# State-space loop of a decoder kernel: a step product in a buffer for each block, the channels' SiLU two units sooner, the first decay ahead, half of the C rows ahead of the locked sum

## The chip, the cores and the metric

The kernel runs on one core of a Trainium2 chip. The time is that of one execution on the device, in microseconds (us). Five engines run side by side, each through its own list of instructions in order, and wait for one another with semaphores: TensorE (PE, matmuls), VectorE (DVE), ScalarE (ACT), GpSimd (POOL) and SyncE (SP, which here only issues DMAs).

## The reference

Two decoder layers on x of 16 x 64 tokens by 256. Each layer is a mixer, a cross attention and a feed-forward part, all with a residual. The change lies in the first mixer alone, a state-space block with 512 channels and 16 states:

```python
zxbcdt = hidden_states @ W_in.T
z, x, Bm, Cm, dtl = jnp.split(zxbcdt, splits, axis=-1)
dt_full = dtl @ W_dt.T + b_dt
delta = jax.nn.softplus(dt_full + b_dt)
...
x = jax.nn.silu(x + conv_b[None, :, None])       # after a causal convolution over 4 steps
...
def step(state, inp):
    u, dlt, Bs, Cs = inp
    dA = jnp.exp(dlt.reshape(b, NC, DPG)[..., None] * A_g)
    du = (dlt * u).reshape(b, NC, DPG)
    state = dA * state + du[..., None] * Bs[:, :, None, :]
    y = jnp.einsum('bgdn,bgn->bgd', state, Cs).reshape(b, D_INNER)
    return (state, y)
...
y = y + x.transpose(0, 2, 1) * D_param
y = y * jax.nn.silu(z)
return y @ W_out.T
```

Here `x` after the SiLU is `u` in the kernel, `dlt` is delta, `dA` the decay, `du` the step product.

## The kernel before

The 512 channels lie in four blocks k = 0 to 3 (`NK`) of 128 partitions; a row of a tile holds all 1024 tokens (`TOK`). The 16 states are walked one at a time (`DST`), so the loop has 64 units u = 16k + n. What one unit does, engine by engine:

- ACT, L637: the decay `m_da` of unit u, exp(delta times a column of `a_log`), in a ring of three buffers; it waits for scan u-3. In three units of a block, n = 4, 9, 14 (`SHARED`), also L643, the `put`: it copies a finished input row into PSUM.
- PE, L1083 (`put_b`): for the other 13 units two selecting matmuls that spread row B of the unit over the partitions into PSUM; `put_b(u+1)` stands in iteration u and waits for scan u-1. L1095 (`add_state`): adds `m_hc` of unit u-2 to the block's y in PSUM banks 4 and 5, with four passes of 512 columns in the profile.
- DVE, L1869: the product B times `m_du` for units that have their own (52 of 64). L1874: the scan over time, h = dA h + input. Scan u waits for `m_hc` of unit u-3, since `m_h` is a ring of three.
- POOL, L468: `m_hc` = h times the row of C. For shared units L473: it multiplies the loaded row B by `m_du`, three units ahead (`m_pd`).
- SP, L318: loads `m_cb`, the unit's rows of C spread over the partitions (512 KB), in a ring of three; the load for unit u is issued when `m_hc` of unit u-3 is done. Shared units also load `m_bb` (512 KB), four units ahead.

Beside this, block k+1 is made ready during block k. PE (L1047, `project`) makes dt in n = 0 and 1 (`steps`), C in n = 3 and 4 (`columns`), the convolution in n = 11 and z of block k in n = 13 and 14. From n = 0 on, all of them but the x columns and the convolution use PSUM banks 6 and 7 in turn. ACT reads dt in L583 and L584 (`step_in`, n = 2, signalled by `m_ax`), then makes the softplus, copies the C rows (L576, n = 6), takes up the convolution (L612, n = 12), computes u by SiLU at the end of n = 15 (L616, `channels`) and right behind it SiLU of z (L668), then loads the exponential's table set again (L553). POOL has the softplus pieces (L434, L438, L444 at n = 12), the step product `m_du` (L452, `step_inputs`, ahead of the `m_hc` of n = 14) and the gate (L458, n = 4 of the next block). DVE adds the skip term after the third scan of the next block (L1850, `skip`); the first `add_state` of that block (L1095, n = 0) waits for it with `m_yd`, since it starts banks 4 and 5 anew. This is the locked sum.

`m_du` is one tile, in `region_c`; `ctxT`, the transposed context for the cross attention behind the loop, is loaded at the start of the program, and `m_rowsT` holds the C rows of a block on their way to DRAM. The order on each engine is the written order; no scheduler changes it. In what follows sum16 means `add_state(16)`, put17 `put_b(17)`, hc13 the `m_hc` of unit 13, and so on; du1 is the step product of block 1.

## Time and profile before

| | us |
|---|---|
| median of 3 runs | 925.9 |
| lowest and highest | 923.86 and 926.99 |
| the profiled execution, its own time | 924.2 |
| its span | 922.3 |
| busy in the span: PE, DVE, ACT, POOL | 822.4, 549.7, 433.7, 302.3 |

The span is what the profiler saw from the first to the last instruction; 1.9 us lie around it. The loop runs from 41.5 us (first scan) to 275.6 us (last scan) of this span, some 25% of it. The large PE share belongs to the stages behind the loop. In a timeline row stand the start, the duration (of a merged group from its first start to its last end), engine, line, operation, written tile and read tiles, and in brackets how long the engine sat idle before and what the profile holds responsible. That releaser is inferred from the last semaphore event, and an instruction waiting for several can be put down to the wrong one. The end of a PE group is modelled; how far apart two groups start is the safer measure.

### The profile page before, as it was taken

The page shows a single profiled execution, that of the slowest core. Times are in us where ns is not written, and L with a number is a line of the kernel's source. Part 1 is how long each engine was busy: PE and PEld are TensorE (multiplying, and loading weights), DVE is VectorE, ACT ScalarE, POOL GpSimd, SP SyncE. Part 2 cuts the span into 40 slices and gives each one's busy share as a digit, 9 for nine tenths or more (in the row PEclk, how much of TensorE's full clock was granted, in tenths as well). Part 3 has the DMA queues.
Part 4 walks back from the last instruction along what each step waited for, and adds up shares of the span by engine and source line. Part 5 has one row for each costly group of instructions (what it writes and reads, how often), then busy time and mean ns, then how long its engine had stood idle before and what let it go on. Part 6 is the DMA issues. An engine that isn't in the chain of part 4 may idle for free.

```text
span 922.3 us, 12515 instructions
## 1 busy us (share of the span) xinstructions
PE 822.4 (89%) x5082; PEld 502.2 (54%) x5082; DVE 549.7 (60%) x666; ACT 433.7 (47%) x650; POOL 302.3 (33%) x148
## 2 busy tenths in 40 slices
PE   6797897986989889999999899998989799989977
PEld 2232342332445456666666676666677466657755
DVE  3799989899895223333424534347792534565686
ACT  2774566545433555555564321233654222232475
POOL 0089999899880000000001001111017993000000
PEclk9889899899899999999999999999999999999999
DMA  9576666656994200000000121405100000000001
GB/s 309 149 190 175 179 163 179 185 173 173 246 229 154 108 1 1 1 1 1 1 1 12 41 92 64 177 18 192 69 3 1 1 1 1 1 1 1 1 1 46
DMA packets 26376, 77.02 MB, mean 84 GB/s; under 512 B 3568, under 2 KB 10480, under 8 KB 25072
## 3 DMA queue, kind: packets, MB, share of 16 engines
q1 hardware_dynamic: 25552, 74.13, 27.4%
q0 software_dynamic: 768, 2.10, 0.7%
q8 instruction: 41, 0.67, 0.3%
q14 instruction: 15, 0.12, 0.0%
HBM read 68.75 MB, written 7.08 MB: 82 GB/s over the span
## 4 chain that ended last, share of the span: by engine, by line
PE 56%; ACT 11%; DVE 11%; DMA 9%; POOL 7%; issue 6%; SPq 0%; POOLq 0%; DVEq 0%; ACTq 0%
PE ps L1297 11%; PE ps L1213 9%; DMA region_b<-m_rows 5%; POOL region_c L468 4%; PE ps L1396 4%; PE ps L1422 4%; PE ps L1285 4%; PE ps L1260 4%; DMA region_c<-m_rows 3%; PE ps L1218 2%; PE ps L1095 2%; PE ps L1047 2%; POOL region_b L468 2%; PE ps L1166 2%; PE ps L1465 2%
## 5 line engine op out<-in xcount | busy, mean ns | idle before, releaser
L1213 PE MATMUL ps<-xnT,region_a 128*128 128x512 f32 x256 | 120.1, 599 | 1.4 <-ACT region_c L718 0.8
L468 POOL TENSOR_TENSOR region_c<-region_c,region_b 128x1024 f32<-128x1024 f32 x42 | 100.9, 2410 | 54.6 <-DMA region_b<-m_rows 47.5
L1095 PE MATMUL ps<-region_c,ident 128*128 128x512 f32 x168 | 90.0, 665 | 17.2 <-POOL region_c L468 11.0
L1874 DVE TENSOR_TENSOR_SCAN region_c<-region_c,ps 128x1024 f32<-128x1024 f32 x43 | 97.9, 2283 | 1.7 <-ACT ps L643 0.4
L489 POOL DMA_INDIRECT f_in<-xn,f_row x8 | 8.0, 995 | 277.2 <-DVE f_row L1985 275.4
L1951 DVE COPY region_b<-ps 128x512 f32<-128x512 f32 x32 | 21.4, 689 | 83.7 <-PE ps L1271 83.6
L1213 PEld LDWEIGHTS ps<-xnT,region_a 128*128 128x128 f32 x256 | 47.2, 190 | 41.2 <-issue 35.8
L1869 DVE TENSOR_TENSOR ps<-ps,region_c 128x1024 f32<-128x1024 f32 x52 | 63.3, 1217 | 10.3 <-PE ps L1083 10.3
L1095 PEld LDWEIGHTS ps<-region_c,ident 128*128 128x128 f32 x168 | 34.2, 212 | 58.0 <-issue 33.6
L1297 PE MATMUL ps<-region_c 128*128 128x256 f32 x256 | 59.8, 380 | 0.0
L1297 PEld LDWEIGHTS ps<-region_c 128*128 128x128 f32 x256 | 48.5, 190 | 16.7 <-issue 11.5
L468 POOL TENSOR_TENSOR region_b<-region_c 128x1024 f32<-128x1024 f32 x21 | 50.6, 2408 | 8.4 <-DVE region_c L1874 5.9
L637 ACT ACTIVATE region_c<-region_c,a_log 128x1008 f32<-128x1008 f32 x43 | 47.9, 1127 | 9.1 <-DVE region_c L1874 9.0
L1095 PE MATMUL ps<-region_b,ident 128*128 128x512 f32 x84 | 44.7, 658 | 8.1 <-POOL region_b L468 6.0
L1874 DVE TENSOR_TENSOR_SCAN region_c<-region_a,ps 128x1024 f32<-128x1024 f32 x21 | 48.0, 2283 | 3.1 <-issue 1.4
L710 ACT ACTIVATE region_c<-ps 128x512 f32<-128x512 f32 x32 | 19.1, 596 | 64.9 <-PE ps L1213 64.9
L1047 PE MATMUL ps<-xnT,region_b 128*128 128x512 f32 (+1 forms) x96 | 47.4, 629 | 0.7 <-ACT xnT L544 0.7
L713 ACT ACTIVATE region_c<-ps 128x512 f32<-128x512 f32 x32 | 19.1, 596 | 57.5 <-PE ps L1213 57.5
L1083 PE MATMUL ps<-region_b,sel_b 96*128 96x512 bf16 x104 | 33.7, 409 | 14.0 <-DVE region_c L1874 14.0
L746 ACT ACTIVATE region_c<-ps 128x512 f32<-128x512 f32 x48 | 25.5, 598 | 35.5 <-PE ps L1285 35.5
L1916 DVE TENSOR_TENSOR region_c<-ps,small 128x1024 f32<-128x1024 f32 x8 | 9.8, 1225 | 54.1 <-PE ps L1260 54.1
L1285 PE MATMUL ps<-region_b,ctxn 64*128 64x256 f32 x256 | 38.4, 433 | 3.7 <-ACT region_c L746 2.5
(252 smaller groups left out, 1636.3 us busy)
## 6 DMA issues: line engine op xcount, KB each, us to landing
region_b<-m_rows SPq DMA_DIRECT2D x43, 512.0 KB, 5.1
region_c<-m_rows SPq DMA_DIRECT2D x21, 512.0 KB, 5.1
xn<-m_brows SPq DMA_DIRECT2D x12, 512.0 KB, 4.3
region_a<-in_x_wo SPq DMA_DIRECT2D x2, 2048.0 KB, 10.9
m_rows<-region_b SPq DMA_DIRECT2D x4, 512.0 KB, 5.5
region_a<-in_x_wq SPq DMA_DIRECT2D x8, 256.0 KB, 7.2
region_b<-in_f_fc SPq DMA_DIRECT2D x1, 2048.0 KB, 7.9
region_b<-in_f_proj SPq DMA_DIRECT2D x1, 2048.0 KB, 13.1
```

What stands on the lines that cost most here:

```text
L468: pool.tensor_tensor(m_hc[u % 3], m_h[u % 3], m_cb[u % 3], ALU.mult).then_inc(sem("m_hc"), 1)
L637: act.activation(m_da[u % 3][:, :, 1:S], m_delta[k % 2][:, :, 1:S], ACT.Exp, scale=a_log[:, k, n:n + 1]).then_inc(sem("m_da"), 1)
L1047: last = pe.matmul(ps[0:rows, pair_at + c, :], lhs(k), (rhs if rhs is not None else xnT[:, k, :])[:, c * HALF:c * HALF + HALF], start=(k = ...
L1095: last = pe.matmul(ps[:, 4 + c, :], ident[:, :], m_hc[u % 3][:, c * HALF:c * HALF + HALF], start=(n == 0), stop=(n == DST - 1))
L1213: last = pe.matmul(b, w, xnT[:, k, cols(it)], start=(k == 0), stop=(k == KH - 1))
L1260: last = pe.matmul(ps[64 * (b % 2):64 * (b % 2) + 64, 4 + a // 2, c:c + S], q_T[:, a, S * b:S * b + S], keys_T[:, S * b:S * b + S], start= ...
L1285: last = pe.matmul(banks[r].rearrange("p (s a q) -> p s a q", s=2, a=4)[:, s], ctxn[64 * r:64 * r + 64, 4 * (it // 4) + 2 * m + s, :], mov ...
L1297: last = pe.matmul(tiles2(2 * (it // 4) + t // 2)[:, t % 2, :], o_Ts[layer][it % 2][:, a, 128 * t:128 * t + 128], wvo[layer][:, 4 * (it % ...
L1396: last = pe.matmul(ps[:, 4 + 2 * (s % 2) + c, :], f_xT[h][:, j, k, :], f_fc[:, bass.ds(weights_at[s] + (HID * k + HALF * c), HALF)], start ...
L1422: last = pe.matmul(ps[:, 2, 0:D], f_aT[s % 2][:, hb, :], f_proj[:, bass.ds(weights_at[s] + D * hb, D)], start=(hb == 0), stop=(hb == HB - 1))
L1869: dve.tensor_tensor(inputs(u), inputs(u), m_du, ALU.mult).then_inc(sem("m_dbu"), 1)
L1874: dve.tensor_tensor_scan(m_h[u % 3], m_da[u % 3].rearrange("p b t -> p (b t)"), inputs(u), 0.0, ALU.mult, ALU.add).then_inc(sem("m_scan"), 1)
```

## The change

1. `m_du` becomes a list of four: blocks 0 and 2 in the old tile, block 1 in `ctxT`, block 3 in `m_rowsT`. So du of the next block no longer waits for this block's last products; block 2 waits for block 0's, block 3 for the last store of C rows.
2. The load of `ctxT` goes from the start of the program to unit (k = 3, n = 2), behind the C rows of that unit.
3. POOL makes du ahead of the `m_hc` of n = 13, not of n = 14.
4. ACT computes u (`channels`) at n = 13, with its own change of tables and back; at n = 15 it makes the first decay of the next block ahead of SiLU of z.
5. PE makes the first half of the C columns at n = 2 ahead of `add_state`, which there is the locked sum; the second half stays at n = 3.

```diff
-        m_du = view("C", 56, [TOK])
+        m_du = [view("C", 56, [TOK]), ctxT[:, :], view("C", 56, [TOK]), m_rowsT]
...
-            load(ctxT[:, :], io["ctxT"], "ld_x0")
...
                     if n == 2:
                         sp.wait_ge(sem("m_delta"), NK)
                         sp.wait_ge(sem("m_u"), NK)
+                        sp.wait_ge(sem("m_pd"), len(SHARED) * (NK - 2))
+                        sp.wait_ge(sem("m_dbu"), own_products(DST * (NK - 2) - 1))
+                        load(ctxT[:, :], io["ctxT"], "ld_x0")
...
             def step_inputs(k):
                 pool.wait_ge(sem("m_u"), k + 1)
                 pool.wait_ge(sem("m_delta"), k + 1)
-                pool.wait_ge(sem("m_pd"), len(SHARED) * k)
-                pool.wait_ge(sem("m_dbu"), own_products(DST * k - 1))
-                pool.tensor_tensor(m_du, m_delta[k % 2].rearrange("p b t -> p (b t)"), m_u[:, k, :], ALU.mult)\
+                if k == 2:
+                    pool.wait_ge(sem("m_pd"), len(SHARED))
+                    pool.wait_ge(sem("m_dbu"), own_products(DST - 1))
+                if k == 3:
+                    pool.wait_ge(sem("st_rows"), 16 * NK)
+                pool.tensor_tensor(m_du[k], m_delta[k % 2].rearrange("p b t -> p (b t)"), m_u[:, k, :], ALU.mult)\
                     .then_inc(sem("m_du"), 1)
...
-                if n == DST - 2 and k < NK - 1:
+                if n == DST - 3 and k < NK - 1:
                     step_inputs(k + 1)
...
+            for u in range(NK * DST):
+                k, n = u // DST, u % DST
+                if n or not k:
+                    decay(u)
...
+                    if n == DST - 3:
+                        channels(k + 1)
+                        exp_tables()
                     if n == DST - 1:
-                        channels(k + 1)
+                        decay(u + 1)
...
+                if n == 2 and k < NK - 1:
+                    pe.wait_ge(sem("m_ax"), k + 2)
+                    columns("C", k + 1, (0,))
                 if u >= 2:
                     add_state(u - 2)
...
-                    if n in (3, 4):
-                        pe.wait_ge(sem("m_ax"), k + 2)
-                        columns("C", k + 1, (n - 3,))
+                    if n == 3:
+                        columns("C", k + 1, (1,))
```

`decay(u)` is the old code of L637 with its waits, put into a function. The products of DVE and POOL name `m_du[k]` in place of `m_du`. Three places show the new order. In the listings a name in brackets is a semaphore that the instruction waits for.

POOL at the end of block 0, from hc11 to the first of block 1; L468 is `m_hc`, L473 the product for a shared unit, L444 the end of delta, L452 du. Before:

```order
L468 TENSOR_TENSOR region_b<-region_c 128x1024 [waits m_y,ld_cb2,m_scan]
L473 TENSOR_TENSOR xn<-xn,region_c 128x1024 [waits ld_bb0,m_du]
L468 TENSOR_TENSOR region_c<-region_c,region_b 128x1024 [waits m_y,ld_cb0,m_scan]
L444 TENSOR_TENSOR region_c<-region_a 128x1024 [waits m_sel]
L468 TENSOR_TENSOR region_c<-region_c,region_b 128x1024 [waits m_y,ld_cb1,m_scan]
L452 TENSOR_TENSOR region_c<-region_c 128x1024 [waits m_pd,m_dbu,m_delta,m_u]
L468 TENSOR_TENSOR region_b<-region_c 128x1024 [waits m_y,ld_cb2,m_scan]
```

In the changed kernel `m_hc` is L473, the shared product L478, the end of delta L446 and du L457:

```order
L473 TENSOR_TENSOR region_b<-region_c 128x1024 [waits m_y,ld_cb2,m_scan]
L478 TENSOR_TENSOR xn<-xn,region_c 128x1024 [waits ld_bb0,m_du]
L473 TENSOR_TENSOR region_c<-region_c,region_b 128x1024 [waits m_y,ld_cb0,m_scan]
L446 TENSOR_TENSOR region_c<-region_a 128x1024 [waits m_sel]
L457 TENSOR_TENSOR ctxT<-region_c 128x1024 [waits m_delta,m_u]
L473 TENSOR_TENSOR region_c<-region_c,region_b 128x1024 [waits m_y,ld_cb1,m_scan]
L473 TENSOR_TENSOR region_b<-region_c 128x1024 [waits m_y,ld_cb2,m_scan]
```

du has changed places with hc13, and hc13 stands behind it.

ACT from the take-up of the convolution (L612) to the first decay of block 1; L637 is the decay, L643 the copy of a shared row, L616 SiLU for u, L668 SiLU of z, L553 the table set of the exponential. Before:

```order
L612 ACTIVATE region_a<-ps,mpar 128x1024 [waits m_proj]
L637 ACTIVATE region_a<-region_c,a_log 128x16x63 [waits m_scan]
L637 ACTIVATE region_c<-region_c,a_log 128x16x63 [waits m_scan]
L643 ACTIVATE ps<-xn 128x1024 [waits m_scan,m_pd]
L637 ACTIVATE region_c<-region_c,a_log 128x16x63 [waits m_scan]
L616 ACT_TABLE_LOAD
L616 ACTIVATE region_c<-region_a 128x1024 [waits m_conv]
L668 ACTIVATE region_c<-ps 128x1024 [waits m_delta,m_yg,m_proj]
L553 ACT_TABLE_LOAD
L637 ACTIVATE region_a<-region_c,a_log 128x16x63 [waits m_scan,m_delta]
```

In the changed kernel these lines are L617, L642, L653, L621, L681 and L558:

```order
L617 ACTIVATE region_a<-ps,mpar 128x1024 [waits m_proj]
L642 ACTIVATE region_a<-region_c,a_log 128x16x63 [waits m_scan]
L621 ACT_TABLE_LOAD
L621 ACTIVATE region_c<-region_a 128x1024 [waits m_conv]
L558 ACT_TABLE_LOAD
L642 ACTIVATE region_c<-region_c,a_log 128x16x63 [waits m_scan]
L653 ACTIVATE ps<-xn 128x1024 [waits m_scan,m_pd]
L642 ACTIVATE region_c<-region_c,a_log 128x16x63 [waits m_scan]
L642 ACTIVATE region_a<-region_c,a_log 128x16x63 [waits m_scan,m_delta]
L681 ACT_TABLE_LOAD [waits m_delta,m_yg]
L681 ACTIVATE region_c<-ps 128x1024 [waits m_proj]
L558 ACT_TABLE_LOAD
```

SiLU for u with a load on either side now stands ahead of the decay and the copy of unit 14, and SiLU of z behind the first decay of block 1.

PE from put19 to put21, in block 1; L1083 is `put_b`, L1095 `add_state`, L1047 the C columns. Before:

```order
L1083 MATMUL ps<-region_b,sel_b 128x512 [waits m_scan]
L1083 MATMUL ps<-region_b,sel_b 128x512
L1095 MATMUL ps<-region_c,ident 128x512 [waits m_yd,m_hc]
L1095 MATMUL ps<-region_c,ident 128x512
L1095 MATMUL ps<-region_b,ident 128x512 [waits m_hc]
L1095 MATMUL ps<-region_b,ident 128x512
L1047 MATMUL ps<-xnT,region_b 128x512 [waits m_ax]
L1047 MATMUL ps<-xnT,region_b 128x512
L1083 MATMUL ps<-region_b,sel_b 128x512 [waits m_scan]
```

In the changed kernel they are L1096, L1108 and L1060:

```order
L1096 MATMUL ps<-region_b,sel_b 128x512 [waits m_scan]
L1096 MATMUL ps<-region_b,sel_b 128x512
L1060 MATMUL ps<-xnT,region_b 128x512 [waits m_ax]
L1060 MATMUL ps<-xnT,region_b 128x512
L1108 MATMUL ps<-region_c,ident 128x512 [waits m_yd,m_hc]
L1108 MATMUL ps<-region_c,ident 128x512
L1108 MATMUL ps<-region_b,ident 128x512 [waits m_hc]
L1108 MATMUL ps<-region_b,ident 128x512
L1060 MATMUL ps<-xnT,region_b 128x512 x2
L1096 MATMUL ps<-region_b,sel_b 128x512 [waits m_scan]
```

One half of C stands ahead of the locked sum and the other ahead of put21, so both halves now stand between put19 and put21, where only one stood. The half that stood between put21 and put22 is gone from there.

## Rows read from the trace of the kernel before

**Rows 1.** Busy time by stretch: us and instructions of each engine, clock, DMA share

```profile
98.40:159.30 60.90, 52.17 (x123) 21.28 (x122) 55.88 (x32) 37.76 (x37) 56.88 (x25) 0.94 0.66 173
...
220.00:282.00 62.00, 51.22 (x136) 23.73 (x135) 56.87 (x37) 23.56 (x22) 48.70 (x21) 0.94 0.93 243
```

**Rows 2.** Timeline of DVE at the block edges and around the locked sum

```profile
91.30 2.26 DVE L1874 TENSOR_TENSOR_SCAN region_c<-region_a,ps 128x1024 f32<-128x1024 f32 x1
...
98.44 1.23 DVE L1869 TENSOR_TENSOR ps<-ps,region_c 128x1024 f32<-128x1024 f32 x1 [1.44 <-PE ps L1083]
...
101.91 1.21 DVE L1869 TENSOR_TENSOR ps<-ps,region_c 128x1024 f32<-128x1024 f32 x1
...
118.05 1.23 DVE L1869 TENSOR_TENSOR ps<-ps,region_c 128x1024 f32<-128x1024 f32 x1 [1.51 <-PE ps L1083]
...
121.92 1.23 DVE L1869 TENSOR_TENSOR ps<-ps,region_c 128x1024 f32<-128x1024 f32 x1 [0.32 <-PE ps L1083]
...
152.13 2.26 DVE L1874 TENSOR_TENSOR_SCAN region_c<-region_c,ps 128x1024 f32<-128x1024 f32 x1
...
159.26 1.23 DVE L1869 TENSOR_TENSOR ps<-ps,region_c 128x1024 f32<-128x1024 f32 x1 [1.43 <-PE ps L1083]
...
220.07 1.23 DVE L1869 TENSOR_TENSOR ps<-ps,region_c 128x1024 f32<-128x1024 f32 x1 [1.41 <-PE ps L1083]
```

**Rows 3.** Timeline of POOL: hc13 and du1, then hc51

```profile
93.56 2.37 POOL L468 TENSOR_TENSOR region_c<-region_c,region_b 128x1024 f32<-128x1024 f32 x1
95.88 2.36 POOL L452 TENSOR_TENSOR region_c<-region_c 128x1024 f32<-128x1024 f32 x1
...
235.75 2.35 POOL L468 TENSOR_TENSOR region_c<-region_c,region_b 128x1024 f32<-128x1024 f32 x1 [1.63 <-PE ps L1095]
```

**Rows 4.** Timeline of PE: sum13 to put21, then the same place at the later edges

```profile
95.99 1.98 PE L1095 MATMUL ps<-region_c,ident 128*128 128x512 f32 x4
97.81 0.60 PE L1083 MATMUL ps<-region_b,sel_b 96*128 96x512 bf16 x2
100.61 3.54 PE L1095 MATMUL ps<-region_b,ident 128*128 128x512 f32 x4 [2.21 <-POOL region_b L468]
103.94 1.21 PE L1047 MATMUL ps<-region_a,region_b 128*128 128x512 f32 x2
...
110.50 3.13 PE L1095 MATMUL ps<-region_c,ident 128*128 128x512 f32 x4 [1.90 <-DVE region_c L1850]
...
115.70 1.88 PE L1047 MATMUL ps<-xnT,region_b 128*128 128x512 f32 x4
117.42 0.60 PE L1083 MATMUL ps<-region_b,sel_b 96*128 96x512 bf16 x2
...
161.44 2.92 PE L1095 MATMUL ps<-region_c,ident 128*128 128x512 f32 x4 [2.21 <-POOL region_c L468]
...
222.24 1.98 PE L1095 MATMUL ps<-region_c,ident 128*128 128x512 f32 x4 [2.21 <-POOL region_c L468]
```

**Rows 5.** Timeline of PE: a group behind 1.78 us of idle time

```profile
70.96 0.61 PE L1083 MATMUL ps<-region_b,sel_b 96*128 96x512 bf16 x2 [1.78 <-DVE region_c L1874]
```

**Rows 6.** Timeline of ACT: units 13 to 15, step_in of block 2, copy of unit 30

```profile
85.02 1.12 ACT L637 ACTIVATE region_c<-region_c,a_log 128x1008 f32<-128x1008 f32 x1
...
89.03 1.03 ACT L643 ACTIVATE ps<-xn 128x1024 f32<-128x1024 f32 x1 [1.86 <-POOL xn L473]
...
91.13 1.28 ACT L616 ACT_TABLE_LOAD   x1
92.42 1.06 ACT L616 ACTIVATE region_c<-region_a 128x1024 f32<-128x1024 f32 x1
...
109.21 1.11 ACT L584 ACTIVATE region_a<-ps,mpar 128x1024 f32<-128x1024 f32 x1
...
149.84 1.03 ACT L643 ACTIVATE ps<-xn 128x1024 f32<-128x1024 f32 x1 [3.41 <-POOL xn L473]
```

**Rows 7.** DMA issues: KB each, median us from issue to landing

```profile
region_b<-m_rows SPq DMA_DIRECT2D x43, 512.0 KB, 5.1
```

8 lines of the change are left out of this document (4 added, 4 removed).

## The prediction

> **What bounds the kernel now.** I began with the busy time by stretch [rows 1]. Between the first products of blocks 1 and 2 DVE is busy for 55.88 of 60.90 us and POOL for 56.88. Both are nearly full, and PE with 52.17 of modelled busy time is not far off. The change touches only the loop, so what it can give lies in the few microseconds in which DVE idles there. The timeline of DVE [rows 2] shows where: 1.44, 1.43 and 1.41 us ahead of the first product of blocks 1, 2 and 3 (I call these places the edges), then 1.51 and 0.32 us ahead of products 21 and 22. Block 2 repeats the last two as 1.51 and 0.32 ahead of products 37 and 38; block 3, which makes no C for a next block, has no such pair.
>
> The releaser in the first of these rows is misleading. put16 was done before sum13 started at 95.99 [rows 4], while du1 on POOL ran from 95.88 to 98.24 [rows 3] and product 16 started at 98.44. The edge waits for du, and du stands behind hc13 in POOL's list. Product 21 starts 0.63 us behind the start of put21 (117.42), and put21 stands behind sum16, sum17 and half a C; this chain starts when the skip term releases sum16 at 110.50 [rows 4]. So the edge belongs to POOL and the second place to PE.
>
> In every sum below I use distances between starts, since the ends on PE are modelled. A group of four passes at full clock takes 1.72 us (C half, 115.70 to 117.42) or 1.82 behind a wait (sum13, 95.99 to 97.81). At the lower clock level sum14 took 3.33 (100.61 to 103.94); the same place at the next edge lasts 2.92 as a row, and 1.98 at the third, where the clock stayed up. A row outlasts the distance by 0.16 to 0.2, so the three prices are 3.33, about 2.7 and 1.82 [rows 4].
>
> **Part 1: du ahead of hc13, with a tile for each block.** The new tiles remove the wait for product 15, which ends where scan 15 starts, some 2.3 before 97.0, and would hold du at its new place. du now starts where hc13 did, at 93.56, and ends at 95.9, ahead of the end of scan 15 at 97.0 (98.44 less 1.44) [rows 2, 3]. The idle 1.44 ahead of product 16 goes, three times, 4.3 us in all. What is late next is hc13: it ends at 98.24 in place of 95.93. Two things wait for it. Scan 16 could start at 98.24, when product 16 is through, so it loses at most 0.1. And PE: sum13 stands ahead of put17 in PE's list. Before, sum13 ran at 95.99 and PE idled for 2.21 us behind put17; now PE idles for some 2.4 us ahead of sum13, and put17 starts at 98.3 plus one group. That is 100.1, 101.0 or 101.6 for the three prices, and product 17 at 0.63 more: 100.7, 101.6 or 102.3. It started at 101.91 [rows 2], so the edge yields +1.2, +0.3 or -0.4 us instead of 1.44. Since 2.4 us of idle time is longer than the 2.21 behind which the clock fell at two edges of three, I take the middle, +0.3, and keep both ends.
>
> hc14 to hc16 keep their places in time. The C rows of unit 16 are asked for when hc13 is done, now 2.3 us later: at about 98.7, landing 5.1 later [rows 7] at 103.8, where POOL would want them at 102.9. POOL then runs 0.9 late, but over the block it idled for 4.0 us [rows 1], and sum16 waits for the skip and not for hc16. Nothing on the path.
>
> **Part 2: SiLU for u two units sooner.** At n = 13 ACT now has, behind the decay of 85.02, a table load 1.28, SiLU 1.06 and a load back 1.28 [rows 6], 3.6 us, ahead of the decay and the copy of unit 14. The cover is ACT's wait of 1.86 for the shared product ahead of that copy. The copy thus ends at about 91.9 instead of 90.06, and scan 14, which started at 91.30 [rows 2], starts at about 92.0: 0.7 late in block 0. In block 1 the wait ahead of the copy is 3.41 [rows 6]: the copy moves by 0.2 to 0.3 and is through at 151.1, scan 30 starts at 152.13 [rows 2]. Nothing is lost there, and block 2 stands alike. In block 0 the 0.7 comes out of the 1.44 that DVE would wait at the edge, so product 17 can't be sooner than 101.1; it costs nothing unless put17 is at its quickest. POOL has u long before du's new place. The Trainium skill, page "ScalarE: Activation LUTs", section "What ACT_TABLE_LOAD costs", adds a drain of about 1380 ns to each load of 1283 ns. This trace shows the 1.28 but no drain: the load starts at 91.13 and SiLU at 92.42 [rows 6]. By the page the copy would be another 2.8 us late; that is a rival below.
>
> **Part 3: the first decay ahead of SiLU of z.** Without it the decay of unit 16 would stand behind SiLU of z and a table load and would be the next wait of scan 16. Now it follows the decay of 15 and is done by about 95. It makes Part 1 possible, no more. SiLU of z has a load of its own again, in the time in which ACT waits for z. Zero.
>
> **Part 4: the C half ahead of the locked sum.** It looks as if 1.9 us of PE's idle time ahead of sum16 took up a group of 1.72. But the half needs `m_ax`, since dt lies in the same banks, and the second instruction of `step_in` runs from 109.21 to 110.32 [rows 6], just when the skip is done too. So the half doesn't go into that idle time as it stands. Moreover both halves now stand ahead of put21: from PE's restart R to put21 there are four groups, 6.9 us at full clock, where three took 6.92 (110.50 to 117.42), for sum16 and sum17 ran in part at the lower level (5.20 from 110.50 to 115.70 against 3.44, 1.8 us too much) [rows 4]. Gain or loss thus hangs on two questions.
>
> When is R? The edge moves it. With sum14 no longer the group behind the wait, the dt halves and `m_ax` come sooner: sum14 starts at about 101.4 and takes 1.72, so it ends at 103.1 in place of 103.94, and the first dt half loses its slow share, 0.2 (a row of 1.21, where half a group and the 0.16 by which rows outlast the distance are 1.02). R is 110.3 less 1.0, 109.3. At the cheap edge it is 108.7, at the dear one 110.0.
>
> And the clock? The idle time ahead of R is 1.7 us. Behind 1.90 the groups ran at the lower level, behind 1.78 at the higher (0.61 for a put, as at full clock) [rows 4, 5]. I take the higher: 109.3 + 6.9 = 116.2 for put21 against 117.42, 1.2 us. As the half is gone ahead of put22, DVE's 0.32 there goes too: 1.5 in block 1. Block 2 is the same with 1.4. These two sums already hold the gain of their edge, because it is PE that releases product 21. With the lower level, 1.8 dearer, each becomes -0.3.
>
> **Part 5: ctxT.** It leaves a time at the start in which nothing behind it was waited for and comes into block 3, where the DMAs are busy for 0.93 of the time at 243 GB/s [rows 1]. 512 KB are 2.1 us there. POOL stands still for 1.63 us at that time [rows 3] (hc51 waits for the skip by way of sum48), so the C rows of unit 52 may be 0 to 0.5 us late; I take 0.3. The waits of SP for it are all over by then.
>
> **The sum.** Block 1 -1.5, block 2 -1.4, edge of block 3 -0.3, ctxT +0.3: -2.9 us. From the profiled execution, 924.2 (its span 922.3), that is 921.3. The median of the runs is 925.9, 1.7 above that execution, so 923.0. About 0.3%, 2.8 us, is what a measurement of this kernel can tell from no change; the forecast lies right on that bound.
>
> **The rivals.** *The clock stays up at the edges too* (for it: the third edge; against: the first two). Then R is 108.7, put21 at 115.6, so 2.2 and 2.3 for the blocks and 1.2 for the third edge: 5.7 less 0.3, and 920.5. *The idle time of 1.7 costs the lower level* (for it: 1.90 did, twice): 0.3 lost in both blocks, the third edge and ctxT cancel, 0.6 slower: 926.5. *The C half is uncovered, slower*: if `m_ax` comes no sooner than before, R stays at 110.3, and at the lower level put21 comes 6.9 + 1.8 later, at 119.0, 1.6 late; 0.3 comes back at product 22. Twice 1.3, with 0.4 lost at the third edge and 0.5 for ctxT: 3.5 slower, 929.4. It decides from the point at which the second half of dt ends no sooner than 108.1 (the first instruction of `step_in`, 1.0, stands between it and 109.21). *A table change dearer than its row*: with a second 1.3 for each load the copies of units 14 and 30 are 2.6 us later, scan 14 is 3.3 and scan 30 some 1.7 late, and the edges can't repay it; about 3 slower, 929. That is the page's case.
>
> **How the numbers follow.** Forecast, R sooner at the higher clock and the edges in part: 0.45, from 921 to 925, half of it beyond the bound. Clock up everywhere: 0.20. Lower level at R: 0.20. Uncovered half: 0.12. Dear tables: 0.02, with 0.01 for anything else. Faster by over 0.3%: 0.23 + 0.20 = 0.43. Slower: 0.11. Within: 0.46. The range reaches to the best rival and beyond the third, 919.8 to 927.5, and leaves out the two slow ones and a little below.
>
> **What would show it.** DVE: no idle time ahead of products 16, 32 and 48, but 0.2 to 1.8 ahead of products 17, 33 and 49, put down to PE. POOL: the du rows ahead of hc13. PE: an idle time of 2.4 ahead of sum13, and of 1.7 ahead of the first C half; two groups for C between put19 and put21. DVE's wait ahead of product 21 still about 1.2 and that ahead of 22 gone. ACT: six table loads more in the loop, scan 14 about 0.7 late and scans 30 and 46 in time. I am wrong if put17 isn't held by sum13, if the first C half starts while PE would have idled before, or if the clock's levels fall otherwise than where the rows of before have them.

## The result, and the profile after

The change made the kernel slightly slower. Over 20 runs each on one chip the changed kernel took 926.92 us in the median and the kernel before 924.73; the ratio is 1.0031, interval 1.0017 to 1.0045. Between the medians lie 2.2 us more, where 2.9 us less was forecast. One execution of the kernel before took 1200.73 us, far from all others, and does not enter the ratio.

| | before | after |
|---|---|---|
| the profiled execution | 924.2 | 922.14 |
| its span | 922.3 | 920.2 |
| busy in it: PE, DVE, ACT, POOL | 822.4, 549.7, 433.7, 302.3 | 814.0, 549.4, 441.7, 302.4 |
| mean granted clock in it | 0.963 | 0.974 |
| first scan to last scan | 231.89 | 230.99 |

The profiled execution of the changed kernel is the quickest of its twenty (922.14 to 933.93), so its trace shows the change at its best: the loop takes 0.9 us less than in the trace of the kernel before, while the medians lie 2.2 us the other way. Even there something is given back. From the last scan to the end the program took from 646 to 654 us in the twenty traces of this document, so spans and loops of single traces are compared with care, and the ratios rest on the many executions.

Busy time by stretch, for blocks 1 and 3 of the changed kernel, from first product to first product and from product 48 on (columns as in [rows 1]):

```profile
96.16:156.46 60.30, 50.40 (x122) 20.63 (x122) 55.69 (x33) 40.36 (x39) 56.85 (x25) 0.97 0.65 174
215.24:277.00 61.76, 50.21 (x130) 22.20 (x131) 53.88 (x33) 24.49 (x23) 50.31 (x22) 0.97 0.96 240
```

Block 1 is 0.6 us shorter than in [rows 1], with the same work on DVE and POOL. In block 3 the share of the DMAs is 0.96 where it was 0.93; the load of ctxT itself now lies there.

DVE of the changed kernel (start, duration; the idle time ahead in brackets): products 16, 17, 21, 22 and 48 with scan 16, which answer to [rows 2], then scans 52, 56, 57 and 62.

```profile
96.16 1.21 DVE L1884 TENSOR_TENSOR ps<-ps,ctxT 128x1024 f32<-128x1024 f32 x1
97.78 2.29 DVE L1889 TENSOR_TENSOR_SCAN region_c<-region_c,ps 128x1024 f32<-128x1024 f32 x1 [0.42 <-POOL region_c L473]
101.37 1.23 DVE L1884 TENSOR_TENSOR ps<-ps,ctxT 128x1024 f32<-128x1024 f32 x1 [1.30 <-PE ps L1096]
...
117.22 1.23 DVE L1884 TENSOR_TENSOR ps<-ps,ctxT 128x1024 f32<-128x1024 f32 x1 [1.43 <-PE ps L1096]
...
120.69 1.21 DVE L1884 TENSOR_TENSOR ps<-ps,ctxT 128x1024 f32<-128x1024 f32 x1
...
215.24 1.21 DVE L1884 TENSOR_TENSOR ps<-ps,region_b 128x1024 f32<-128x1024 f32 x1
...
231.69 2.29 DVE L1889 TENSOR_TENSOR_SCAN region_c<-region_c,ps 128x1024 f32<-128x1024 f32 x1 [0.84 <-ACT ps L653]
...
247.32 2.29 DVE L1889 TENSOR_TENSOR_SCAN region_c<-region_a,ps 128x1024 f32<-128x1024 f32 x1 [1.88 <-ACT region_a L642]
251.13 2.29 DVE L1889 TENSOR_TENSOR_SCAN region_c<-region_c,ps 128x1024 f32<-128x1024 f32 x1 [1.52 <-ACT ps L653]
...
268.60 2.29 DVE L1889 TENSOR_TENSOR_SCAN region_c<-region_a,ps 128x1024 f32<-128x1024 f32 x1 [1.40 <-ACT ps L653]
```

The edges' waits are gone and so is the 0.32 ahead of product 22. Product 48 starts 4.8 us sooner than before (220.07). Then come waits that the kernel before does not have: scans 52, 57 and 62 wait for the copy (L653) of a shared row, 0.84 + 1.52 + 1.40 = 3.8 us.

POOL of the changed kernel at the first edge: du1, hc13, then hc16, hc17 and the shared product of unit 20. Below it the third edge: hc48 and hc49 as one row, then the shared product of unit 52.

```profile
92.99 2.35 POOL L457 TENSOR_TENSOR ctxT<-region_c 128x1024 f32<-128x1024 f32 x1
95.31 2.34 POOL L473 TENSOR_TENSOR region_c<-region_c,region_b 128x1024 f32<-128x1024 f32 x1
...
104.19 2.35 POOL L473 TENSOR_TENSOR region_c<-region_c,region_b 128x1024 f32<-128x1024 f32 x1 [1.91 <-DMA region_b<-m_rows]
106.50 2.35 POOL L473 TENSOR_TENSOR region_b<-region_c 128x1024 f32<-128x1024 f32 x1
108.80 2.37 POOL L478 TENSOR_TENSOR xn<-xn,ctxT 128x1024 f32<-128x1024 f32 x1
...
223.64 4.65 POOL L473 TENSOR_TENSOR region_c<-region_c,region_b 128x1024 f32<-128x1024 f32 x2 [2.29 <-PE ps L1108]
228.26 2.34 POOL L478 TENSOR_TENSOR xn<-xn,region_b 128x1024 f32<-128x1024 f32 x1
```

And the kernel before at its third edge: hc48, hc49 and the same shared product.

```profile
224.47 2.34 POOL L468 TENSOR_TENSOR region_c<-region_c,region_b 128x1024 f32<-128x1024 f32 x1
227.14 2.35 POOL L468 TENSOR_TENSOR region_c<-region_c,region_b 128x1024 f32<-128x1024 f32 x1 [0.34 <-DVE region_c L1874]
229.45 2.35 POOL L473 TENSOR_TENSOR xn<-xn,region_c 128x1024 f32<-128x1024 f32 x1
```

Before, hc48 started 3.1 us behind the start of scan 48 (221.33), right behind hc47, and no edge had a wait for a DMA. After, hc48 starts 6.8 us behind scan 48 (216.83), and the shared product of unit 52 stands 11.4 us behind that scan instead of 8.1. The 2.29 ahead of hc48 is put down to PE, which had long been done; the same instruction at the first edge is put down to its C rows. The copy of unit 52 on ACT follows the shared product, and scan 52 follows the copy.

### The profile page after: what moved, and what is told of

Its sections match the earlier page's. It is cut to its first block, busy times and chain, and to the rows that moved or that the text cites. A ratio compares the mean times of both kernels' runs of the same rounds, so it can differ in the third digit from the quotient of the medians.

```text
span 920.2 us, 12520 instructions
## 1 busy us (share of the span) xinstructions
PE 814.0 (88%) x5082; PEld 496.6 (54%) x5082; DVE 549.4 (60%) x666; ACT 441.7 (48%) x656; POOL 302.4 (33%) x148
## 4 chain that ended last, share of the span: by engine, by line
PE 52%; ACT 8%; DVE 8%; DMA 6%; issue 2%; POOL 1%; another core or an unknown queue 0%; SPq 0%; DVEq 0%; ACTq 0%; POOLq 0%
PE ps L1312 11%; PE ps L1228 9%; PE ps L1411 4%; PE ps L1437 4%; DMA region_b<-m_rows 4%; PE ps L1275 4%; PE ps L1300 4%; PE ps L1233 2%; DMA region_c<-m_rows 2%; PE ps L1181 2%; PE ps L1286 1%; PE ps L1480 1%; ACT region_c L759 1%; PE ps L1533 1%; PE ps L1189 1%
## 5 line engine op out<-in xcount | busy, mean ns | idle before, releaser
L473 POOL TENSOR_TENSOR region_c<-region_c,region_b 128x1024 f32<-128x1024 f32 x42 | 100.8, 2407 | 55.0 <-DMA region_b<-m_rows 45.9
L1108 PE MATMUL ps<-region_c,ident 128*128 128x512 f32 x168 | 85.9, 638 | 19.8 <-POOL region_c L473 16.0
L1108 PEld LDWEIGHTS ps<-region_c,ident 128*128 128x128 f32 x168 | 31.5, 197 | 59.0 <-issue 29.5
L642 ACT ACTIVATE region_c<-region_c,a_log 128x1008 f32<-128x1008 f32 x43 | 48.2, 1129 | 15.3 <-DVE region_c L1889 10.6
L473 POOL TENSOR_TENSOR region_b<-region_c 128x1024 f32<-128x1024 f32 x21 | 50.5, 2404 | 6.3 <-DMA region_c<-m_rows 2.9
L1060 PE MATMUL ps<-xnT,region_b 128*128 128x512 f32 (+1 forms) x96 | 48.5, 640 | 4.2 <-ACT region_a L589 3.5
L1096 PE MATMUL ps<-region_b,sel_b 96*128 96x512 bf16 x104 | 32.6, 398 | 16.9 <-DVE region_c L1889 16.9
L1108 PE MATMUL ps<-region_b,ident 128*128 128x512 f32 x84 | 41.1, 611 | 6.0 <-POOL region_b L473 5.9
L1953 DVE TENSOR_TENSOR region_c<-region_c 128x1024 f32<-128x1024 f32 x8 | 9.8, 1222 | 46.9 <-ACT region_c L718 46.9
```

What stands on the lines that cost most here:

```text
L473: pool.tensor_tensor(m_hc[u % 3], m_h[u % 3], m_cb[u % 3], ALU.mult).then_inc(sem("m_hc"), 1)
L642: act.activation(m_da[u % 3][:, :, 1:S], m_delta[k % 2][:, :, 1:S], ACT.Exp, scale=a_log[:, k, n:n + 1]).then_inc(sem("m_da"), 1)
L1060: last = pe.matmul(ps[0:rows, pair_at + c, :], lhs(k), (rhs if rhs is not None else xnT[:, k, :])[:, c * HALF:c * HALF + HALF], start=(k = ...
L1108: last = pe.matmul(ps[:, 4 + c, :], ident[:, :], m_hc[u % 3][:, c * HALF:c * HALF + HALF], start=(n == 0), stop=(n == DST - 1))
```

## The experiments

Every kernel computes the whole reference, and every ratio is against the kernel before on the same chip, from 12 executions of the kernel and 23 to 35 of the kernel before (20 each for the first); the interval is one of 95%. Kernels of one set ran on one chip and are to be compared within it. "Lag" is the DVE time in front of scans 52, 57 and 62 put down to the copy of a shared row, in the one traced execution; the last column is in us, of that execution too.

| set, kernel | ratio | interval | lag | first to last scan |
|---|---|---|---|---|
| the changed kernel | 1.0031 | 1.0017 to 1.0045 | 3.76 | 230.99 |
| 1 after_again | 1.0044 | 1.0020 to 1.0069 | 0 | 233.74 |
| 1 ctxt_behind | 1.0017 | 0.9992 to 1.0042 | 1.37 | 235.51 |
| 1 c_in_place | 1.0030 | 1.0003 to 1.0057 | 0.65 | 235.22 |
| 1 before_ctxt_late | 1.0000 | 0.9976 to 1.0025 | 0.52 | 229.08 |
| 2 after_fence | 1.0029 | 1.0009 to 1.0048 | 0 | 230.94 |
| 2 before_fence | 0.9995 | 0.9977 to 1.0012 | 0 | 229.92 |
| 2 after_fence_ctxt_behind | 1.0002 | 0.9979 to 1.0025 | 2.79 | 231.36 |
| 2 du_in_place | 0.9988 | 0.9969 to 1.0007 | 0 | 227.82 |
| 3 du_in_place_again | 0.9988 | 0.9970 to 1.0007 | 0 | 231.09 |
| 3 cb_first | 0.9995 | 0.9976 to 1.0014 | 0 | 227.91 |
| 3 cb_first_ctxt_behind | 0.9989 | 0.9971 to 1.0007 | 1.03 | 229.60 |
| 3 du_and_c_in_place | 0.9999 | 0.9980 to 1.0018 | 0.31 | 230.32 |
| 4 after_third | 1.0015 | 0.9988 to 1.0042 | 2.33 | 235.90 |
| 4 cb_first_again | 0.9974 | 0.9950 to 0.9998 | 0 | 229.74 |
| 4 before_cb_first | 0.9983 | 0.9957 to 1.0009 | 0.47 | 229.75 |
| 4 du_in_place_cb_first | 0.9974 | 0.9945 to 1.0003 | 0 | 228.08 |
| 5 after_fourth | 1.0023 | 1.0002 to 1.0045 | 5.09 | 233.31 |
| 5 after_fence_again | 1.0025 | 1.0008 to 1.0043 | 4.08 | 233.43 |

The letters in an expectation are that set's own names for the theories that it weighs.

### Set 1: the load of ctxT, the C half

after_again is the changed kernel unaltered. The edits of the others:

```diff
 # ctxt_behind: the changed kernel, ctxT loaded behind the loop
-                        sp.wait_ge(sem("m_pd"), len(SHARED) * (NK - 2))
-                        sp.wait_ge(sem("m_dbu"), own_products(DST * (NK - 2) - 1))
-                        load(ctxT[:, :], io["ctxT"], "ld_x0")
...
+            load(ctxT[:, :], io["ctxT"], "ld_x0")
             load(wvT, io["x0_wvT"], "ld_x0")
```

```diff
 # c_in_place: the changed kernel, both C halves where they were
-                if n == 2 and k < NK - 1:
-                    pe.wait_ge(sem("m_ax"), k + 2)
-                    columns("C", k + 1, (0,))
...
-                    if n == 3:
-                        columns("C", k + 1, (1,))
+                    if n in (3, 4):
+                        pe.wait_ge(sem("m_ax"), k + 2)
+                        columns("C", k + 1, (n - 3,))
```

```diff
 # before_ctxt_late: the kernel before, ctxT loaded in unit (3, 2)
-            load(ctxT[:, :], io["ctxT"], "ld_x0")
...
                         sp.wait_ge(sem("m_u"), NK)
+                        load(ctxT[:, :], io["ctxT"], "ld_x0")
```

> The changed kernel once more, to see how its executions spread. Theory L (the load of ctxT in block 3 makes the C rows late, and that eats the gain): 1 to 4 us slower than before, with DVE idle for some 3 to 6 us in block 3 ahead of scans 52 to 62, whatever the clock does. Theory K (the higher clock of the trace shown, 0.974, was luck): other executions have a mean granted clock near 0.965, and lower-level groups behind the idle time ahead of the first C half, which cost 1 to 2 us in blocks 1 and 2. Both can hold together.

> The changed kernel with the load of ctxT moved out of block 3 to just behind the loop, ahead of the load of wvT. Theory L: 3 to 5 us faster than the changed kernel, so 1 to 3 us faster than before; the C rows of block 3 land 5 to 7 us after their issue as before and not 8 to 9. Theory K: no different from the changed kernel within 1 us.

> The changed kernel with both C halves at n = 3 and 4 behind the locked sum, as before. Theory K: 1 to 3 us faster than the changed kernel, if the half ahead of the sum is what costs. Theory L: equal to it, or up to 1 us slower, since the two kernels make product 21 wait by about the same (three groups at the lower clock level or four at the higher).

> The kernel before with only one thing changed: ctxT is loaded at unit (k = 3, n = 2), behind the C rows. Theory L: 2 to 4 us slower than before. Theory K: equal to before within 1 us.

The loss came again, 1.0044. Without the 512 KB in block 3 some of it may be missing (1.0017, with overlapping intervals), yet the same load does nothing that can be measured to the kernel before (1.0000). The C half in its old place does not undo the loss either (1.0030). So neither is the cause alone.

The traces of after_again, ctxt_behind and c_in_place have one predicated copy on DVE of 8.0 us where the others take 3.4. It lies beside POOL. Here is the plainest case, from after_third, a later run of the changed kernel: DVE's copy, then POOL's instructions beside it (hc42 and hc43 in one row, the shared product of unit 46, hc44).

```profile
199.86 8.02 DVE L1861 COPY_PREDICATED region_a<-region_a,region_b 128x1024 f32<-128x1024 uint32 x1 [0.57 <-POOL region_b L440]
```

```profile
199.69 4.65 POOL L473 TENSOR_TENSOR region_c<-region_c,region_b 128x1024 f32<-128x1024 f32 x2
204.31 2.35 POOL L478 TENSOR_TENSOR xn<-xn,region_c 128x1024 f32<-128x1024 f32 x1
211.40 2.36 POOL L473 TENSOR_TENSOR region_b<-region_c 128x1024 f32<-128x1024 f32 x1 [4.75 <-DVE region_c L1889]
```

POOL runs from 199.69 to 206.66 without a gap, and the copy ends 1.2 us behind that. Was this the cause?

### Sets 2 and 5: no copy beside POOL

```diff
 # after_fence, after_fence_again, before_fence; with the edit of ctxt_behind: after_fence_ctxt_behind
+                if n == 11 and k < NK - 1:
+                    pool.wait_ge(sem("m_sel"), k + 1)
                 pool.wait_ge(sem("m_scan"), u + 1)
```

`m_sel` is signalled by the copy, so POOL starts hc11, hc27 and hc43 only when the copy is through.

> The changed kernel, and POOL waits ahead of the m_hc of n = 11 until DVE's predicated copy is done. Theory P (the copy reads three SBUF operands and shares a port with POOL; when it misses the gap between two POOL instructions it waits for three of them and takes 8.0 us and not 3.4, and that is what makes typical executions of the change slower): no copy of 8 us in the trace, 1.5 to 3 us faster than the changed kernel, so 0 to 1 us slower than before or faster, and a smaller spread. Rival Q (the long copies are rare and the kernel before has as many; the change is slower for its C rows and tables): equal to the changed kernel, 2 to 3.5 us slower than before.

> The kernel before with the same wait of POOL for the copy. Theory P, if only the change brings the long copies: equal to before within 1 us. If the kernel before has them too, 1 to 2 us faster than before. Rival Q: as the latter.

> The changed kernel with POOL's wait for the copy, and ctxT loaded behind the loop. Theory P with the C rows of block 3 costing too: the fastest of the set, 2 to 4 us faster than before. If the load of ctxT costs nothing once the copies are short: equal to after_fence. Rival Q: 1 to 2 us slower than before, as without the wait.

> The changed kernel beside the next one on one chip: 1.0015 to 1.0045 of before, as the three times before. Its trace may have one copy of 8.0 us where the others have 3.4.

> The changed kernel with POOL waiting for the predicated copy ahead of hc11, so that no copy can run against it. If the late C rows cost their time mainly at the edges and behind them, it is level with after_fourth within 0.12%. If they cost it mainly through the long copies (4.6 us each, in most executions), it is 0.25 to 0.4% below after_fourth.

The nine copies in the fenced traces with du early all take 3.4 us. The loss stays: 1.0029, and 1.0025 beside 1.0023 of the unfenced kernel on one chip. So keeping the long copies away does not bring the time back. They occur in 4 of 18 copies in the unfenced traces with du early and the loads in their order, in none of 9 with the C rows issued first, and in none of 21 with du in its old place or in the kernel before without the fence.

That does not clear the long copies of every share. From scan 14 to product 49 the two unfenced traces of the changed kernel that hold one take 134.04 and 133.94 us (after_again, after_third), the two without take 128.69 and 128.42 (the first one, after_fourth): some 5.4 us less. But the three fenced traces take 130.97 to 131.32 there. In them PE idles 2.8 us ahead of sum13, sum29 and sum45, where it idles 2.5 to 2.6 otherwise, so the fence seems to have a price of its own with du early; in the kernel before it has none (0.9995). And the late C rows cost time without a long copy as well: after_fourth has no long copy and 5.09 us of lag, while after_again has one and no lag. How the loss is divided between the two stays open.

### Sets 2 and 3: du back behind hc13, and the C rows sooner

```diff
 # du_in_place, du_in_place_again; with the edit of c_in_place: du_and_c_in_place
-                if n == DST - 3 and k < NK - 1:
+                if n == DST - 2 and k < NK - 1:
                     step_inputs(k + 1)
```

```diff
 # cb_first, cb_first_again; with the edit of ctxt_behind: cb_first_ctxt_behind
+                load(m_cb[u % 3], m_rows[k][8 * n:8 * n + 8].partition_broadcast(DST), f"ld_cb{u % 3}")
                 if u + 4 < NK * DST and shared(u + 4):
...
                     load(m_bb[j % 2], m_brows[u + 4:u + 5].partition_broadcast(128), f"ld_bb{j % 2}")
-                load(m_cb[u % 3], m_rows[k][8 * n:8 * n + 8].partition_broadcast(DST), f"ld_cb{u % 3}")
```

In units 16, 32 and 48 SP issues the shared row of the unit four ahead, and behind it the C rows. Both wait for the `m_hc` of three units before, which is hc13, hc29 and hc45: the very instruction that du was put in front of.

> The changed kernel with du on POOL ahead of the m_hc of n = 14, as before; tiles, tables, decay and C halves as changed. My sum gave the edges about 0.3 us each and the rest to the C halves, so 1 to 2 us slower than the changed kernel if nothing else counted. If du's place is what brings long copies (theory P in its narrow form): no copy of 8 us, and 1 to 2 us faster than the changed kernel.

> du in its old place once more, on the chip of the runs beside it. Theory D (making du two positions sooner makes hc13 and with it the load of the next block's first C rows 2.3 us late; POOL waits for them at every edge, 1.9 to 2.5 us, and that is the loss): 1 to 3 us faster than before again, 3 us faster than the changed kernel; in the trace no POOL wait for C rows at the edges, and a loop of 228 us or so. Rival N (the earlier result was the chip's spread): equal to before or slower.

> The changed kernel, with the load of a unit's C rows issued ahead of the load of the shared B row, where both come in one unit (among them the first unit of each block). It takes 512 KB and one issue out of the way of the late C rows and keeps du sooner. Theory D: POOL's wait of 1.9 to 2.5 us at the edges falls to under 1, and the kernel is 1.5 to 3 us faster than the changed one, about equal to before. Rival R (the loss comes from PE, where sum13 holds put17 back, and not from the C rows): equal to the changed kernel within 1 us, with DVE still waiting ahead of products 17, 33 and 49.

> As cb_first, and ctxT loaded behind the loop. Theory D with DMA time short in block 3: 3 to 4 us faster than the changed kernel, 1 us faster than before. Rival R: 1 to 2 us slower than before, as with ctxT behind alone.

> du and both C halves in their old places; what is left of the change is the tiles, the tables, the decay ahead and the late ctxT. By my sum for the C halves (1.2 us in each of two blocks when the clock stays up, a loss of 0.3 when it falls): 0 to 2.5 us slower than with du alone in place. These edits without du sooner and without the C half should be worth nothing by themselves: equal to before within 1 us.

The rest of the change, without du early, is at 0.9988 twice. The unfenced changed kernel did not run on that chip; against after_fence, which did, du_in_place is 0.41% faster by the means (interval 0.19 to 0.63%), of which the fence may account for a part. du_and_c_in_place came 1.1 us behind du_in_place_again by the means, inside the noise and inside what was expected, and level with the kernel before. du_in_place, POOL with hc17 and the shared product of unit 20, then DVE with products 16 and 21, then PE with the first C half and put21:

```profile
104.96 2.35 POOL L473 TENSOR_TENSOR region_b<-region_c 128x1024 f32<-128x1024 f32 x1 [0.40 <-DVE region_c L1889]
107.28 2.36 POOL L478 TENSOR_TENSOR xn<-xn,ctxT 128x1024 f32<-128x1024 f32 x1
```

```profile
97.82 1.23 DVE L1884 TENSOR_TENSOR ps<-ps,ctxT 128x1024 f32<-128x1024 f32 x1 [1.42 <-PE ps L1096]
...
115.67 1.23 DVE L1884 TENSOR_TENSOR ps<-ps,ctxT 128x1024 f32<-128x1024 f32 x1 [0.58 <-PE ps L1096]
```

```profile
108.06 1.99 PE L1060 MATMUL ps<-xnT,region_b 128*128 128x512 f32 x4 [1.77 <-ACT region_a L589]
...
115.03 0.60 PE L1096 MATMUL ps<-region_b,sel_b 96*128 96x512 bf16 x2
```

The edge's 1.42 is back, and still product 21 comes 1.55 us sooner than in the changed kernel (117.22), though scan 14 started within 0.2 us in both (90.69 and 90.53). That last gain is not there in every execution: du_in_place_again has scan 14 at 90.68 and product 21 at 117.35, behind a wait of 2.28 us, and its loop took 231.09 us where 228 was expected. What both traces share is that POOL no longer waits for C rows at the edges, that there is no lag in block 3, and no long copy.

The landing times of the rows at the edges show why. In the kernel before, the C rows of units 16, 32 and 48, issued behind the shared row, took 6.1, 5.7 and 5.8 us and landed 0.3 to 0.7 us ahead of the `m_hc` that reads them. There was no more slack than that. In all nine traces with du early and the loads in their order they took 5.9 to 6.7 us, from a later issue, and each of the 27 `m_hc` started 0.12 or 0.13 us behind the landing.

cb_first keeps du early and reaches the same end by another way: the C rows no longer stand behind 512 KB of shared row, and in its three traces they land in 4.4 to 4.7 us. Its POOL at the same places, from cb_first_again: hc16, hc17, the shared product of 20; then hc48, hc49, the shared product of 52.

```profile
102.70 2.35 POOL L473 TENSOR_TENSOR region_c<-region_c,region_b 128x1024 f32<-128x1024 f32 x1 [0.29 <-DMA region_b<-m_rows]
106.40 2.34 POOL L473 TENSOR_TENSOR region_b<-region_c 128x1024 f32<-128x1024 f32 x1 [1.35 <-DMA region_c<-m_rows]
108.70 2.37 POOL L478 TENSOR_TENSOR xn<-xn,ctxT 128x1024 f32<-128x1024 f32 x1
...
221.87 2.35 POOL L473 TENSOR_TENSOR region_c<-region_c,region_b 128x1024 f32<-128x1024 f32 x1
225.57 2.34 POOL L473 TENSOR_TENSOR region_c<-region_c,region_b 128x1024 f32<-128x1024 f32 x1 [1.35 <-DMA region_b<-m_rows]
227.87 2.36 POOL L478 TENSOR_TENSOR xn<-xn,region_b 128x1024 f32<-128x1024 f32 x1
```

hc48 starts 4.7 us behind scan 48 (217.22) where it took 6.8, but hc49 now waits, and the shared product still stands 10.7 us behind that scan against 11.4. In part the lateness has only moved: product 49 waits 1.49 us for PE in this trace, so DVE comes to scan 52 later too, and finds the copy made. But no lag appears later in the block either. The loop in two stretches shows where each kernel gains and loses, in us; a star marks a trace with a long copy, and all of those lie in the first stretch.

| | scan 14 to product 49 | product 49 to the last scan |
|---|---|---|
| the kernel before | 132.24 | 49.82 |
| the changed kernel, four traces | 128.69, 134.04*, 133.94*, 128.42 | 52.83, 50.09, 52.49, 53.28 |
| cb_first, cb_first_again | 129.86, 130.33 | 48.57, 49.92 |
| du_in_place, du_in_place_again | 129.53, 132.88 | 48.73, 48.74 |

The changed kernel gains more than 3 us in the first stretch unless a long copy falls into it, and then gives back up to 3.5 in the second; the other two kernels gain less in the first (du_in_place_again nothing) and give back nothing in the second, or 0.1. (The second stretch of the kernel before is one trace; with the loads in the other order, or with ctxT late, that kernel took 47.61 and 47.67.) The high DMA share of block 3 is not enough by itself to bring the lag: in du_in_place it is 0.99 there (215.5 to 277 us) and the C rows land in 7.6 and 6.5 us, and nothing waits for the copies. So undoing either the place of du or the order of the loads takes the loss away. Since both remedies also come without long copies, their times do not say how much of it was the rows' wait and how much the copies.

With the loads in that order, moving ctxT away brings no more (0.9989 beside 0.9995).

### Set 4: all on one chip

before_cb_first is the kernel before with the order of cb_first; du_in_place_cb_first has both edits.

> The changed kernel once more, beside the next three on one chip. Theory D (du ahead of hc13 delays the next block's first C rows by 2.3 us, for which POOL then waits at every edge): 1.003 to 1.004 of before, and 0.3 to 0.4% above cb_first_again on the same chip; the trace has hc16, hc32 and hc48 behind waits of 1.9 to 2.5 us for the C rows. Theory X (the earlier difference was between chips, not between kernels): level with cb_first_again within 0.15%.

> The changed kernel with the load of the C rows issued ahead of that of the shared B rows in each unit. Theory D: 0.999 to 1.0005 of before as the first time (0.9995), and hc16, hc32 and hc48 without a wait of 1.9 us for a DMA. Theory X: level with after_third.

> The unchanged kernel with that order of the two loads alone. Theory D: the kernel before waits for no C row at an edge, so there is nothing to gain, 0.999 to 1.001. A rival G (the order helps by itself, wherever it stands, and cb_first gained by that and not by the removed wait at the edges): 0.996 to 0.997, as much below before as cb_first lies below the changed kernel.

> The change with du behind hc13 as before, and the C rows issued ahead of the shared row. Theory D: both remedies take away the same wait, so they don't add: 0.998 to 0.9995, level with du_in_place (0.9988 twice). If they work on different waits (rival G): 0.995 to 0.996.

The changed kernel is 0.38% slower than cb_first_again (means 923.85 and 920.37 us, interval 0.15 to 0.62%), so the loss is the kernel's and not a chip's. Against the kernel before, all four came lower than was expected of them: 1.0015 where 1.003 to 1.004 stood, and the other three below their ranges too. The two remedies don't add: du_in_place_cb_first and cb_first_again lie within 0.02% of one another (interval 0.23% to either side), as they should if they take the same loss away. The order alone in the kernel before gives 0.9983, which the interval does not tell from nothing, and it is less than half of the 0.38%; but the interval is wide enough that a part of what cb_first gains may be the order's own and not the removed wait. What du in its old place shows does not depend on that: the changed kernel stands at 1.0031, 1.0044, 1.0015 and 1.0023 in its four measurements, and du_in_place, twice, at 0.9988. Of all versions cb_first_again and du_in_place_cb_first lie lowest, 0.26% below the kernel before; only for the first does the interval leave out 1, barely, and the same kernel stood at 0.9995 in set 3. That a version beats the kernel before is thus not shown.

## Why the prediction was wrong

The forecast was 923.0 us, 2.9 less than before; the median came to 926.92, 2.2 more than the kernel before beside it. Two steps of the sum failed. The late C rows of Part 1, put down as "Nothing on the path", come with a loss that turned the sign, and the level of the clock at the first edge took 1 us out of Part 4.

**The edges (Part 1) and the C half (Part 4).** The waits ahead of products 16, 32 and 48 went, product 17 waits for put17 (1.30), and PE idles ahead of sum13. PE at the first edge and at its restart, which answers to [rows 4]:

```profile
97.71 2.77 PE L1108 MATMUL ps<-region_c,ident 128*128 128x512 f32 x4 [2.56 <-POOL region_c L473]
100.27 1.06 PE L1096 MATMUL ps<-region_b,sel_b 96*128 96x512 bf16 x2
101.12 2.41 PE L1108 MATMUL ps<-region_b,ident 128*128 128x512 f32 x4
...
109.61 1.98 PE L1060 MATMUL ps<-xnT,region_b 128*128 128x512 f32 x4 [1.77 <-ACT region_a L589]
...
116.58 0.60 PE L1096 MATMUL ps<-region_b,sel_b 96*128 96x512 bf16 x2
```

Scan 14 started 0.77 us sooner than before, so 0.77 is added to compare. sum13 took 2.56 from start to start, the middle price as taken. But the lower level went on: put17 took 0.85 and sum14 2.25, where the forecast had 1.72 for sum14. That is the term of Part 4 that was mis-sized. So the restart R lies at 110.4 against 110.5, not 1.0 sooner, and put21 at 117.35 against 117.42, not 1.2 sooner. R behind 1.77 us of idle time was at full clock, as forecast, and so it was in blocks 1 and 2 of all eleven traces with du and the C half early. In block 1 the gain up to product 22 is 0.5 us and not 1.5. The third edge, forecast at 0.3, gave 0.9 (product 49 follows product 48 by 3.98 us instead of 3.47, and the wait of 1.41 is gone). From scan 14 to product 49 the profiled execution gained 3.55 us (219.22 + 0.77 against 223.54) where the forecast had 3.2. That agreement is luck: the parts were wrong, and of the three other traces of the changed kernel only after_fourth gained there (3.8), while the two with a long copy lost 1.7 and 1.8.

What the C half is worth hangs on the level of the clock at R, as the forecast said, and is not settled. du_in_place comes to R at 108.06, is at full speed, and product 21 waits 0.58. du_in_place_again comes to the same place behind the same idle time and is at the lower level:

```profile
108.04 2.83 PE L1060 MATMUL ps<-xnT,region_b 128*128 128x512 f32 x4 [1.78 <-ACT region_a L589]
```

Product 21 then waits 2.28. Of the six places of this kind in the three traces with du late and the C half early, two were at full speed and four at the lower level. By time, the C half early or late makes no difference that can be told from nothing, neither with du early (1.0044 and 1.0030) nor with du late (0.9988 and 0.9999).

**The C rows (Part 1), where the forecast failed.** It said that the C rows of unit 16 would be asked for 2.3 us later, that POOL would run 0.9 late, that it idled for 4.0 us in a block, and "Nothing on the path". The delay was seen, but mis-sized and then dismissed. The wait is 1.91 us at the first edge and 2.29 at the third: the 5.1 us of [rows 7] is a median over the loop, while at the edges the shared row is issued just ahead of the C rows, and there they took 6.0, 6.0 and 6.4 us (and 6.1, 5.7 and 5.8 in the kernel before, whose trace was at hand). And POOL's idle time doesn't lie where the delay falls; only hc17 or hc49 stands between the late instruction and the shared product of unit 20 or 52, without a gap. In block 1 this does not reach DVE: scan 20 waits 0.45 us in both kernels. In block 3 it does. The landing times of C rows there, 222 to 280 us (issues, KB each, median us to landing), with ctxT's own:

```profile
region_b<-m_rows SPq DMA_DIRECT2D x9, 512.0 KB, 7.6
region_c<-m_rows SPq DMA_DIRECT2D x4, 512.0 KB, 7.5
...
ctxT<-in_ctxT SPq DMA_DIRECT2D x1, 512.0 KB, 8.4
```

From product 49 to the last scan the changed kernel takes 52.83 us (219.22 to 272.05) and the kernel before 49.82 (223.54 to 273.36): 3.0 lost where 0.3 was forecast. In other executions, as in the one of after_third, a long copy comes on top. That du's place brings this loss is shown by the runs that undo it; the steps from the late rows to each wait in block 3, and why the long copies come with du early, are read from traces and not tested one by one.

**ctxT (Part 5).** In the kernel before it costs nothing that can be measured (1.0000, interval 0.9976 to 1.0025), in keeping with the 0.3. With du early it is 0.0027 of the time by the ratios in two sets (1.0044 against 1.0017, 1.0029 against 1.0002), 1.4 and 1.7 us by the means, each time with overlapping intervals.

**SiLU, tables, first decay (Parts 2 and 3).** ACT of the changed kernel, table load, SiLU, load back, decay of unit 14:

```profile
83.83 1.28 ACT L621 ACT_TABLE_LOAD   x1
85.12 1.06 ACT L621 ACTIVATE region_c<-region_a 128x1024 f32<-128x1024 f32 x1
86.19 1.28 ACT L558 ACT_TABLE_LOAD   x1
87.49 1.14 ACT L642 ACTIVATE region_a<-region_c,a_log 128x1008 f32<-128x1008 f32 x1
```

Each successor starts 1.29 to 1.30 us behind the start of a load, so the dear loads of the rival do not exist here. The Trainium skill, page "ScalarE: Activation LUTs", section "What ACT_TABLE_LOAD costs", adds a drain of about 1380 ns; the trace disagrees. Scan 14 was not 0.7 late, as Part 2 had it: it follows scan 13 by 2.2 us in both kernels. ACT took up the convolution 1.6 us sooner (81.67 + 0.77 against 84.01), so SiLU and its two loads ended at 87.47, ahead of the end of the shared product of unit 14 (88.22), and the copy was not held up.

**What was not looked for.** Ahead of the predicated copy that precedes product 12 of block 0 DVE waited 1.14 us for POOL (L438) in the kernel before and 0.45 in the changed one. The six traces with the C half in its old place have 1.09 to 1.41 there, the fourteen with it early 0.45 to 0.59. So the C half moves something far from where it stands. It is no gain that lasts, though: from the first scan to scan 14 those six traces take 49.25 to 50.01 us and the fourteen 49.46 to 51.61.

**The rivals.** None of the four was it. The second, the lower level at R, gave 926.5, close to the measured 926.92, but by luck: its condition did not occur in any trace of the changed kernel. The one that ended on the slow side through the C half was named for the wrong instruction; the C rows' lateness had no chance of its own, though its first sentence stood in Part 1.

## What to carry to other kernels

An instruction that is moved ahead of another delays everything that the other one releases, and a DMA issue among these must be followed to its landing at that very unit, with what is issued ahead of it, not by the median of all units. Idle time summed over a block is no cover: count the instructions between the delay and the next one that somebody waits for. Where a load is needed first, issue it first; here that order was worth as much as undoing the move. And one trace is one execution: the clock and the long copies differed from trace to trace of the same kernel by more than the change was worth.

## What the runs showed of the hardware

A predicated copy of DVE over 128x1024 took 1.35 us where POOL was idle (34.90 in the changed kernel's trace), 3.4 in the loop as a rule, and 8.0 at times. The usual case, in the changed kernel, DVE and then POOL:

```profile
80.31 3.42 DVE L1861 COPY_PREDICATED region_a<-region_a,region_b 128x1024 f32<-128x1024 uint32 x1 [0.45 <-POOL region_b L440]
```

```profile
80.15 2.33 POOL L473 TENSOR_TENSOR region_c<-region_c,region_b 128x1024 f32<-128x1024 f32 x1
82.45 3.45 POOL L473 TENSOR_TENSOR region_b<-region_c 128x1024 f32<-128x1024 f32 x1
```

The copy ends 1.25 us behind the end of POOL's first instruction, and POOL's next one is 1.1 us longer than usual. That reads as if the copy ran between the two, and each held the other off. In the long case POOL's three instructions keep their 2.3 us and the copy ends 1.2 us behind the third. The Trainium skill, page "SBUF — State Buffer", section "SBUF: two separate sides", describes an exclusive lock on a shared port pair, between a DVE instruction with two inputs in SBUF and a POOL instruction that reads SBUF: whoever starts first holds it for the whole instruction. The traces agree, with an addition: the one that waits does not always get its turn when the holder's instruction ends. In 4 of 18 copies it missed two turns.

C rows of 512 KB landed in 5.1 us in the median over the loop of the kernel before, and from 222 to 280 us in 5.9 and 6.3 (the two tiles that hold them); in the changed kernel they took 7.6 and 7.5 there. Issued right behind another load of 512 KB they took 5.7 to 6.7 us at the edges of the kernel before and of the nine traces with du early, and ahead of it 4.4 to 4.7 in those of cb_first.

The clock level that PE had behind an idle time differed from place to place, and the length of that time did not decide it. Behind 1.77 or 1.78 us ahead of the first C half PE was at full speed (2.4 GHz) in all 22 places of the eleven traces with du early, whatever the level a few groups earlier; with du in its old place it was at full speed in two places and at the lower level (1.2 GHz) in four. In block 1 of du_in_place and of du_in_place_again, the same kernel, the groups ahead of it were at full speed in both, and the level behind it was the higher in one and the lower in the other. Behind 2.21 us at the first edge du_in_place was at full speed and the kernel before at the lower level [rows 4].
